# A gated delta rule layer on one core: output with tokens on partitions, both halves of an inverse grown by direct products, paired kk products

## The reference

```python
beta = sigmoid(x @ w_b) * 2.0
g = -exp(A_log) * softplus(x @ w_a + dt_bias)
q, k, v = (conv_silu(x @ w, conv) for w, conv in ...)   # causal, 4 taps
q, k = l2norm(q), l2norm(k)
# per token, per head:
S = S * exp(g_t)
delta = (v_t - k_t @ S) * b_t
S = S + outer(k_t, delta)
o_t = (q_t * 64 ** -0.5) @ S
# then
rms = o * rsqrt(mean(o * o, axis=-1) + EPS)             # over the 128 values of a head
y = (rms * norm_w * silu(x @ w_g)) @ w_out              # w_out sums over all heads
x = x + layernorm(y)
```

## Time and profile before

| | |
|---|---|
| median of 3 runs | 5447.15 us (5446.64 to 5448.37) |
| the profiled execution | 5446.22 us |
| its span, first to last instruction | 5445.0 us |
| busy share PE / DVE / ACT / POOL | 96% / 85% / 55% / 55% |
| delta rule phase, first product to last addition | 144.65 to 4969.3 us |
| before it (norm, gates) | to 128.7 us and the change of phase |
| behind it (experts) | 4970.7 us to the end |

### The profile page before, as it was taken

One profiled execution on the slowest core, in us unless ns is written; L12 is line 12 of the kernel. 1 busy time (PEld: TensorE's weight loads), 2 busy tenths in 40 slices (PEclk: granted clock), 3 DMA queues, 4 the chain that ended last, 5 costly groups with the idle time before them and its releaser, 6 DMA issues. The chain is left out here.

```text
span 5445.0 us, 144552 instructions
## 1 busy us (share of the span) xinstructions
PE 5217.2 (96%) x43532; PEld 3837.1 (70%) x43532; DVE 4620.5 (85%) x10938; ACT 3001.3 (55%) x7772; POOL 2971.6 (55%) x3857
## 2 busy tenths in 40 slices
PE   6899999999999999999999999999999999996998
PEld 6577777777777777777777777777777777774554
DVE  5688888888888888888888888888888888885776
ACT  1456656566566566566566566566665665662221
POOL 3455555555555555565565555555555555553443
PEclk9899999999999999999999999999999999998998
DMA  3111011011011011011110110111110110100110
GB/s 132 40 38 37 27 44 37 27 37 42 29 37 37 27 44 37 28 37 36 36 37 28 40 40 27 37 37 35 37 37 27 42 39 27 37 29 23 39 39 31
DMA packets 114337, 203.67 MB, mean 37 GB/s; under 512 B 12377, under 2 KB 70882, under 8 KB 114274
## 3 DMA queue, kind: packets, MB, share of 16 engines
q1 hardware_dynamic: 114274, 202.90, 11.0%
HBM read 185.56 MB, written 17.30 MB: 37 GB/s over the span
## 5 line engine op out<-in xcount | busy, mean ns | idle before, releaser
L647 DVE SCALAR_TENSOR_TENSOR cv<-ps_a,wqkv,cv 128x511 f32<-128x511 f32 (+2 forms) x1536 | 1115.7, 740 | 21.6 <-ACT cv L640 21.3
L632 PE MATMUL ps_a<-xin,wqkv 128*128 128x512 f32 x2048 | 1011.1, 616 | 48.2 <-issue 28.5
L843 POOL TENSOR_TENSOR bm<-bat,mask 128x256 f16<-128x256 f32 x1536 | 1034.5, 689 | 0.0
L1063 POOL TENSOR_TENSOR rms<-msq,minus_half 128x2 f32<-128x2 f32 x512 | 359.8, 703 | 1065.0 <-DVE msq L1055 1064.9
L904 DVE TENSOR_TENSOR tt<-tt,b 128x256 f16<-128x256 f16 x1536 | 624.5, 414 | 209.5 <-PE b L898 197.1
L914 ACT CAST tt<-b 128x256 f16<-128x256 f32 x1536 | 546.4, 374 | 435.9 <-PE b L909 435.9
L892 ACT ACTIVATE m<-b 128x256 f16<-128x256 f32 x1536 | 549.1, 385 | 308.9 <-PE b L887 308.8
L838 POOL TENSOR_TENSOR tt<-bat,first 128x512 f16<-128x512 f32 x256 | 297.0, 1160 | 757.0 <-DVE tinv L937 756.9
L640 ACT ACTIVATE cv<-ps_a,wqkv 128x512 f32<-128x512 f32 x512 | 351.9, 687 | 546.5 <-PE ps_a L632 546.5
L898 PEld LDWEIGHTS b<-tt,m 128*128 128x128 f16 x6144 | 348.2, 101 | 422.8 <-issue 347.4
L1070 PE MATMUL cz<-wout,yy 128*128 128x256 f32 x2048 | 568.3, 400 | 0.0
(11 more groups left out here) (202 smaller groups left out, 11852.6 us busy)
## 6 DMA issues: line engine op xcount, KB each, us to landing
xin<-xT_scratch SPq DMA_DIRECT2D x128, 512.0 KB, 3.6
grow<-g_scratch SPq DMA_DIRECT2D x128, 512.0 KB, 4.3
gam<-g_scratch SPq DMA_DIRECT2D x256, 96.0 KB, 2.8
n_x<-in_x SPq DMA_DIRECT2D x16, 512.0 KB, 3.3
xT_scratch<-n_xT SPq DMA_DIRECT2D x16, 512.0 KB, 2.6
e_x<-in_x SPq DMA_DIRECT2D x16, 512.0 KB, 4.1
out_y<-e_yo SPq DMA_DIRECT2D x16, 512.0 KB, 2.9
wqkv<-in_w_qkv SPq DMA_DIRECT2D x32, 128.0 KB, 3.4
```

Source lines behind the costliest of these rows:

```text
L632: ins = pe.matmul(ps[:], wqkv[:, k, j * P:(j + 1) * P], xin[p][:, k, :], start=k == 0, stop=k == KT - 1)
L647: s.done(dve.scalar_tensor_tensor(y[:, r:], ps[:, 0:T - r], tap[:, j, TAPS - 1 - r:TAPS - r], y[:, r:], ALU.mult, ALU.add), f"a_tap{j}{r}")
L843: s.done(pool.tensor_tensor(half_of(bm[:, l, units(g), :], l, 1), half_of(bt[:, units(g), :], l, 1), half_of(c["mask"][:, l, :].unsqueeze( ...
```

## The change

- `c_O` swaps its operands, so that its output has tokens on partitions. `c_sq` is then two ACT squares, each of one head, with a running sum along the row into `msq`; the `c_ss` products go. `c_m` and `c_p` are both on POOL. `c_y` multiplies each head with its own `rms` and the gate, `c_yT` transposes both heads on PE (into the second half of bank `co`), `c_yTe` copies on ACT, and `c_out` sums both heads in PSUM, in a bank of `ps_a`. One addition, `c_acc`, is left of two operations.
- The gate is computed with tokens on partitions too: `b_g` has eight matmuls of 256 columns instead of four of 512.
- `norm_w` and its constant go into w_out once, in the gates phase: all of w_out is loaded, scaled on POOL and stored to `wo_scratch`.
- A level of the inverse has the products `b_M`, `b_V` and `b_U`. `b_V` gives the new half of the transpose directly and is added by DVE (`b_Ve`). `b_U` writes a bank of its own, `bu`, shared by both groups; with ones on the diagonal of `m1` it holds the whole new half and is copied by ACT (`b_Ue`). `b_Tp` and `b_Te` go.
- `b_F` also adds the matrix itself by a product with the identity, and `b_T` is a copy on ACT instead of an addition on DVE.
- `b_kk` of a group is one step: for each chunk the products of both row halves follow each other.
- `ck` and `cz` become one bank, `cs`. Bank `co` is now held from `c_O` to `c_yTe`.
- The order of a slot is written anew.

```diff
-    c_y0.3 b_sq1.2 a_proj0.1 a_tap13.1 b_gend.2 b_Me00.2 b_U00.2 c_ss0.3 b_Ue00.2 b_Me51.3 b_n1.2 c_KS1.3 b_U51.3
...
+    b_kT.1 b_V40.2 b_U11.2 a_tap32.1 b_Ve11.2 c_yTe1.3 c_SU2.3 a_tap33.1 b_bm31.2 b_sq0.1 c_O2.3 b_Ve40.2 b_M21.2
+    b_n0.1 b_Ue11.2 b_bm41.2 c_S2.3 a_tanh3.1 b_U40.2 a_silu3.1 b_lo0.2 b_M50.2 b_Me21.2 b_Me50.2 b_Ue40.2 c_sq2.3
+    b_V21.2 c_KS3.3 c_m2.3 b_U21.2 b_ss.1 b_Ve21.2 b_V50.2 c_out1.3 c_R3.3 b_Ue21.2 b_Ve50.2 c_p2.3 b_M31.2 c_Z3.3
+    b_U50.2 c_acc0.3 c_acc1.3 b_rc.1 b_P0.2 c_y2.3 b_kk0.1 b_gam.1 c_u3.3 b_w1.1 b_R0.2 b_kw.1 b_ktok.1 c_yT2.3
+    b_Ue50.2 b_Me31.2 b_ev00.1 b_V31.2 b_Ve31.2 b_ev01.1 b_F0.2 b_bm51.2 c_yTe2.3 b_U31.2 b_Ue31.2 b_root.1 b_qT.1
+    b_eps.2 b_sq1.1 c_O3.3 c_sq3.3 c_out2.3 c_acc2.3 b_diag0.1 c_m3.3 b_t20.1 c_p3.3 b_kk1.1 b_M41.2 b_T0.2 b_n1.1
+    c_Z0.2 b_Me41.2 b_vT0.1 b_bm00.1 c_u0.2 b_ev10.1 b_Tq0.1 b_U41.2 b_hi0.1 b_V41.2 b_Ue41.2 b_vtok0.1 a_proj0
+    c_y3.3 b_Tf0.1 b_Ve41.2 b_M00.1 b_M51.2 c_yT3.3 b_ev11.1 b_vT1.1 b_vtok1.1 b_bm10.1 b_Me00.1 c_SU0.2 b_V00.1
+    b_U00.1 b_Ve00.1 b_Me51.2 c_yTe3.3 b_V51.2 c_out3.3 c_O0.2 b_Ve51.2 c_S0.2 b_Ue00.1 b_M10.1 a_cv0 b_P1.2
+    b_U51.2 c_sq0.2 b_Ue51.2 c_acc3.3 c_KS1.2 a_tap01 b_Me10.1 a_proj1 b_gend.1 b_R1.2 b_F1.2 a_tap02 b_V10.1
+    c_R1.2 b_sel c_m0.2 c_p0.2 b_U10.1 a_tap03 b_E0 b_diag1.1 a_cv1 c_y0.2 a_tanh0 b_g0.1 b_Ue10.1 b_t21.1 c_Z1.2
+    c_yT0.2 b_T1.2 b_bm20.1 b_Ve10.1 a_tap11 a_silu0 a_tap12 b_tg0.1 b_Tq1.1 b_M20.1 b_bm01.1 c_u1.2 b_bm30.1
+    a_tap13 a_proj2 b_Tf1.1 b_Me20.1 b_U20.1 b_kqs.1 b_sg0.1 a_tanh1 a_silu1 c_yTe0.2 b_V20.1 c_SU1.2 a_cv2 b_M01.1
+    b_Ue20.1 b_bm40.1 c_O1.2 b_Ve20.1 a_tap21 a_tap22 b_M30.1 b_Me01.1 c_S1.2 b_E1 b_g1.1 b_bm50.1 b_V01.1 b_Me30.1
+    a_tap23 c_sq1.2 b_Ve01.1 b_U30.1 b_tg1.1 b_V30.1 b_Ve30.1 c_m1.2 a_tanh2 b_bm11.1 a_proj3 b_hi1.1 b_M40.1
+    b_Ue30.1 c_p1.2 c_KS2.2 b_sg1.1 a_silu2 a_cv3 c_y1.2 c_R2.2 b_Me40.1 b_M11.1 b_U01.1 b_Ue01.1 c_out0.2 c_Z2.2
+    c_yT1.2 b_lo1.1 b_Me11.1 b_V11.1 a_tap31 c_u2.2 b_bm21.1
...
+        nc.sync.dma_start(wo[:], w_out.rearrange("n p h d -> p n (h d)")).then_inc(s_wo, 16)
+        nc.sync.dma_start(normw[:], norm_w).then_inc(s_wo, 16)
+        nc.gpsimd.wait_ge(s_wo, 32)
+        nc.gpsimd.tensor_scalar(wo[:], wo[:], normw[:, 0:1], 0.5 * DV ** 0.5, ALU.mult, ALU.mult).then_inc(s_ws, 1)
...
+        nc.sync.wait_ge(s_ws, 1)
+        nc.sync.dma_start(wo_dram.rearrange("n p h d -> p n (h d)"), wo[:]).then_inc(s_out, 16)
+        nc.sync.wait_ge(s_out, 32)
...
+            [(f"b_U{l}{g}", f"b_Ue{l}{g}") for l in range(NLEV) for g in range(2)],
+            [(f"c_KS{m}", f"c_R{m}") for m in range(1, CH)] + [(f"c_Z{m}", f"c_u{m}") for m in range(CH)]
+            + [(f"c_SU{m}", f"c_S{m}") for m in range(CH - 1)],
+            [(f"c_O{m}", f"c_yTe{m}") for m in range(CH)],
...
+                    for m in range(2):
+                        t = slice((2 * n + m) * P, (2 * n + m + 1) * P)
+                        for k in range(KT):
+                            ins = pe.matmul(ps_b[:, m * 2 * DV:(m + 1) * 2 * DV], xin[p][:, k, t], wg[:, k, :],
+                                            start=k == 0, stop=k == KT - 1)
...
+                        for k in range(2):
+                            rows = slice(k * DK, (k + 1) * DK)
+                            ins = pe.matmul(ps_a[k][:, n * 2 * P:(n + 1) * 2 * P], kq[p][rows, 1 - p, t],
+                                            kq[p][rows, :, t], start=True, stop=True)
...
+                    if (yield f"b_V{l}{g}"):
+                        s.need(pe, i, f"b_Me{l}{g}", f"b_Ue{l - 1}{g}" if l else f"b_t2{g}")
+                        for k in range(4):
+                            u = 4 * g + k
+                            ins = pe.matmul(half_bank(bank, l)[:, k], tt[:, 1, u, :], half_of(m1[:, l], l, 0)[:, u],
                                             start=True, stop=True)
...
+                        s.done(dve.tensor_tensor(even, even, half_bank(bank, l), ALU.add), f"b_Ve{l}{g}")
...
+                        pe.matmul(bank[:, k * P:(k + 1) * P], r16[:, u, :], tt[:, 1, u, :], start=True, stop=False)
+                        ins = pe.matmul(bank[:, k * P:(k + 1) * P], tt[:, 0, u, :], c["ident16"][:], start=False,
+                                        stop=True)
...
+                    if (yield f"b_U{l}{g}"):
+                        s.need(pe, i, f"b_Me{l}{g}", f"b_Ue{l - 1}{g}" if l else f"b_t2{g}")
+                        free(pe, i, f"b_U{l}{g}")
...
+                        s.done(act.copy(half_of(tt[:, 1, units(g), :], l, 1), half_bank(bu, l)), f"b_Ue{l}{g}")
...
+                                pe.matmul(co[:, e], kqs[p][:, q_in, m - 1, :], state[:, h, :], start=True, stop=False)
+                            ins = pe.matmul(co[:, e], at[:, 2 * m + h, :], uu[:, h, :], start=m == 0, stop=True)
...
+                    for h in range(2):
+                        ins = act.activation(sqo[:, h, :], out[:, h * DV:(h + 1) * DV], ACT.Square, accum_out=col(msq, h))
...
+                    s.done(pool.tensor_tensor(rms[:, both], msq[:, both], epsq[p][:, both], ALU.add), f"c_m{m}")
...
+                        ins = dve.scalar_tensor_tensor(yy[:, h, :], out[:, e], col(rms, h), sg[p][:, m, e], ALU.mult,
+                                                       ALU.mult)
...
+                        ins = pe.transpose(turned[:, h * P:(h + 1) * P], yy[:, h, :], c["ident"][:])
...
+                        ins = pe.matmul(ps_a[m % 2][:, 0:D], yT[:, h, :], wo[:, h, :], start=h == 0, stop=h == 1)
...
+                    s.done(dve.tensor_tensor(a, a, ps_a[m % 2][:, 0:D], ALU.add), f"c_acc{m}")
...
+        for l in range(NLEV):
+            odd = lambda t: t.rearrange("p u (b k r) -> p u b k r", k=2, r=2 << l)[:, :, :, 1, :]
+            ident = c["ident16"][:].unsqueeze(1)
+            for u in range(NU):
+                ins = pool.tensor_copy(odd(m1[:, l, u:u + 1, :]), odd(ident))
```

More of the change, by code:

```diff
@@ L63 @@
[L63 to L67, removed]
@@ L470, in __init__ @@
                 before = []
+                self.turn.setdefault(first, []).append(before)
                 for d in range(1, 3 * len(users) + 1):
@@ L474, in __init__, with phase_delta @@
                     before.append((LAG[first] - LAG[other[0]] + wraps, other[1]))
-                self.turn[first] = before
     def free(self, eng, i, name):
[L479 to L485, removed]
+        for before in self.turn[name]:
+            for shift, last in before:
+                if not isinstance(i, int) or 0 <= i + shift < NIT:
+                    self.s.need(eng, i + shift, last)
+                    break
+def phase_delta(nc, c, w_qkv, w_gate, wo_dram, xT_dram, g_dram, gate_tok, acc):
     with Phase(nc) as ctx:
@@ L557, in phase_delta @@
         for g in range(2):
[L558 removed]
+            for name in ("b_M", "b_Me", "b_V", "b_Ve", "b_U", "b_Ue", "b_bm"):
                 s.series(f"{name}.{g}", [f"{name}{l}{g}" for l in range(NLEV)])
[L560 to L561 removed]
         for j in range(4):
@@ L567, in phase_delta @@
             s.series(name, [f"{name}{m}" for m in range(CH - 1)])
-        for name in ("c_Z", "c_u", "c_O", "c_sq", "c_y", "c_ss", "c_out", "c_m", "c_p", "c_acch", "c_acc"):
+        for name in ("c_Z", "c_u", "c_O", "c_sq", "c_m", "c_p", "c_y", "c_yT", "c_yTe", "c_out", "c_acc"):
             s.series(name, [f"{name}{m}" for m in range(CH)])
-        sp.dma_start(normw[:], norm_w).then_inc(s.sem("normw_in"), 16)
         def load_x(i, b, par):
@@ L933, in invert @@
                     s.done(ins, f"b_F{g}")
                 if (yield f"b_T{g}"):
-                    s.need(dve, i, f"b_F{g}")
-                    s.need(dve, i - 2, f"c_Z{2 * g + 1}")
-                    s.done(dve.tensor_tensor(tinv[p][:, units(g), :], tt[:, 1, units(g), :], in_units(bank), ALU.add),
-                           f"b_T{g}")
+                    s.need(act, i, f"b_F{g}")
+                    s.need(act, i - 2, f"c_Z{2 * g + 1}")
+                    s.done(act.copy(tinv[p][:, units(g), :], in_units(bank)), f"b_T{g}")
@@ new lines, in emit @@
+                if (yield f"c_m{m}"):
+                    s.need(pool, i, f"c_sq{m}", "b_eps")
+                    s.need(pool, i - 1, f"c_y{m}")
+                    s.done(pool.tensor_tensor(rms[:, both], msq[:, both], epsq[p][:, both], ALU.add), f"c_m{m}")
+                if (yield f"c_p{m}"):
+                    s.need(pool, i, f"c_m{m}")
+                    s.done(pool.tensor_tensor(rms[:, both], rms[:, both], c["minus_half"][:, 0:2], ALU.pow), f"c_p{m}")
+                if (yield f"c_y{m}"):
+                    s.need(dve, i, f"c_p{m}", f"b_sg{m // 2}")
@@ L1042, in emit @@
-                if (yield f"c_ss{m}"):
+                        s.need(dve, i - 1, f"c_yT{CH - 1}")
+                    for h in range(2):
+                        e = slice(h * DV, (h + 1) * DV)
+                        ins = dve.scalar_tensor_tensor(yy[:, h, :], out[:, e], col(rms, h), sg[p][:, m, e], ALU.mult,
```

(8 more changed lines are left out.)

219 lines of the change are left out of this document (89 added, 130 removed).

## The result

The changed kernel takes 5516.7 us (median of 4 runs, 5516.0 to 5521.6) against 5446.9 for the kernel before beside it: a ratio of 1.0131, 95% interval 1.0113 to 1.0148. It is 1.3% slower, with an interval clear of 1, and the forecast of 5278 is missed, outside the range. With 24 waits a trip fewer on ACT, and every operation as in the changed kernel, the same code takes 5267. What the prediction left out is not an operation but the program itself: ACT's part of the loop body came to be fetched from memory again in each trip of the loop (a trip is two iterations, since the code is written out for both parities; there are 61).

The account below looks back on a forecast made before the run. PE's stream was taken to bound the kernel: terms of -1.53 us an iteration, 196 us in 128, and +27 us once give 5446.2 - 196 + 27 = 5277, so 5278 as the runs' median; range 5195 to 5395.

Parts of the forecast that it names:

- the part on the other engines: DVE, ACT and POOL per iteration: 29.4, 26 or so and 22.3 us, all beside PE's stream and priced at nothing.
- PE waits at c_O for the copy yTe: Sign of being wrong: PE waits over 1 us an iteration, above all at c_O for yTe.
- the output chain holding co: Rival: co, held longer, delays the next c_O and all behind it; 5533 us at 2 us late, chance 0.07.
- the four hand-offs: Handing co to the next c_O: 3 us of queueing allowed at the tightest; decisive if together 1.3 us late an iteration.
- The rival of the clock: Rival: added PE transposes lower the clock; 1.2 GHz for a tenth of the loop costs about 450 us, chance under 0.01.
- DVE didn't set the pace: Rival, here denied: DVE and not PE sets the pace, so time follows DVE's 3.6 us to 5012, chance 0.02.
- The rival of the waits: Rival: PE's waits eat most of the gain, leaving 0.1 to 1.0 us an iteration; 5345 to 5440 us, chance 0.17.
- Kk, sums, transposes and identity: Terms on PE's stream per iteration: paired kk -1.15, sums of squares -1.76, transposes of yy +0.88, identity in b_F +0.48 us.
- more than the stream: Rival: PE's old 0.45 us of waits also go, conditions cost nothing, early stages grow by 10 only; 5190 us, chance 0.10.
- the inverse's products: Term on PE's stream: 12 levels keep 12 matmuls of 64 columns for each product, so nothing changes.
- a term of its own: PE's wait at c_O3 for uu goes, -0.39 us an iteration; its counterpart at b_V21 adds +0.39, up to +0.8.
- Once: Stages before the loop: w_out load 8, later store 9, copies into m1 10; together +27 us, from 10 to 45.

Follow-up runs that it names:

- e5: The changed kernel, loop untouched, with 70 long-met waits (35 instructions) on ACT ahead of the first slot: 5268.3 us.
- e2: The changed kernel with the copy b_Ue waiting only for the later of its two products, ACT's body 261 instructions instead of 285: 5267.3 us.
- e7: e2 with the gate rows grow issued ahead of the load of wo in SP's queue: 5238.9 us.
- e4: The kernel before with 96 long-met waits a trip added on ACT, its body 273 instructions instead of 225: 5465.3 us.
- e9: The kernel before with the 96 waits a trip of e4 and 204 more (102 instructions) on ACT ahead of the first slot: 5597.3 us.
- e12: The changed kernel with 20 long-met waits (10 instructions) on ACT ahead of the first slot, where e5 has 70: 5399.5 us.

## Why the prediction was wrong

**The step that failed** is in the part on the other engines: ACT goes from 22.5 us an iteration to 26 or so, lies beside PE's stream, and is priced at nothing. The operations were priced rightly: 315 records of the addition into acc, four an iteration, make 78.8 iterations in the 3000 us, and ACT's 2006.76 us are 25.5 in each. The instructions were not counted, waits and register operations among them, and no step of the working asked whether a loop body is still held when it grows. That step is worth +248 us (e5 against the changed kernel, with the same loop in both), and it turns -180 into +70.

The Trainium skill (Runtime: NRT & Kernel Launch, Instruction fetch mechanics) would have given the warning: it says that a taken branch whose target isn't in the present window of two pages of 16 KiB forces a fetch before the engine can go on. The runs agree on the stall and on its place behind the branch. They differ in grain: here the packets have 8 KB, a body of 285 instructions (18 KB) fell out of what the skill gives as 32 KiB, and one of 312 on DVE did not.

**The signs and the rivals.** "PE waits at c_O for the copy yTe" came as written, with "over 1 us an iteration" (192 us idle in 78.8 iterations are 2.4). The rival that it stood for, the output chain holding co, named the victim and not the culprit; its price of 5533 is near the result for another reason. With the fetches off (e2), no wait of c_O for yTe is left in the view, so the four hand-offs stay within the 3 us that were allowed. The rival of the clock, in with slower at under 0.01, was looked for in the transposes. The clock did fall, behind the standstill of each trip, and took up to 2 of the 4.0 us between 75.2 and 71.2. DVE didn't set the pace either: in e2 it is busy 84% of the time, and the iteration is 35.6 us and not near DVE's 30. The rival of the waits is priced at 5345 to 5440, but its own lower waste of 0.1 us gives 5446 - 13 + 27 = 5460; e2 lies below both.

**The stream.** e2 is the change without the fetches, and its 35.6 us an iteration stand against a forecast of 35.8, its 5267 against 5278. But the terms are off in both directions. The distances from each record's start to the next on PE, summed by line over 80 iterations of the kernel before and 72 of e2 (all of 1000 to 4000 us but the long trips), in us an iteration (a wait counts with the record ahead of it):

```
                          before   e2     by this   forecast
kk                         3.19    2.13    -1.06     -1.15
c_ss                       1.78    -       -1.78     -1.76
yT transposes              -       0.96    +0.96     +0.88
identity in b_F            -       0.45    +0.45     +0.48
M, U and Tp / M, V and U   5.61    4.76    -0.85      0
c_out (wait of kk behind)  3.78    4.69    +0.91      0
b_vT                       1.12    0.87    -0.25      0
all                       37.29   35.60    -1.69     -1.53
```

Kk, sums, transposes and identity are right within 0.1; kk is two blocks of 1.07 us as said (2176.63 to 2177.70), a yT group 0.22 (2166.24 to 2166.46). Two things were not foreseen. The order's new bank sharing lets b_kk1 wait for DVE's c_acc2, 0.83 us an iteration in the waits view and 0.99 by the starts; I had counted waits for b_V and c_O, but not gone through the new list of banks for first users right behind last ones. On the other side, waits of the kernel before went. The first a_proj of a trip came 0.61 us late (the "issue" line of the earlier trace rows), 0.30 an iteration, and a U group behind b_vT 0.21 late; neither does in e2. The working left these to a rival, *more than the stream*.

The line of the inverse's products needs care, for it holds waits of other steps. U took 2.12 us in the kernel before, where 12 groups of 0.12 are 1.44, but 0.39 of the rest is c_O3 waiting for uu behind the last U. The forecast has that as a term of its own, and its counterpart came as written: in e2 b_V21 comes 0.41 us late behind b_M21, forecast 0.39. What else the line lost, beside the wait of a_proj, are steps of about 0.1 us each from an f16 group to an f32 group, fewer now (those into kk the forecast has in its first line). So the inverse's products themselves changed nothing, as forecast; whether its shorter chain bought anything, no run shows. The unforeseen wait and the unforeseen gains nearly cancel, so that 35.8 came out right by some luck.

**DVE and POOL.** DVE is at 30.1 us an iteration (2375.73 in 78.8), foreseen 29.4. Additions into acc take 419 ns, c_y 337 where I had 0.32 us, b_T on ACT 588 instead of 0.62 us:

```profile
L1075 DVE SCALAR_TENSOR_TENSOR yy<-co,rms,sg 128x128 f32<-128x128 f32 x630 | 185.9, 337 | 16.1 <-POOL rms L1066 16.1
...
L1058 ACT ACTIVATION_READ_ACCUMULATOR sqo<-co 128x1 f32 x632 | 133.8, 212 | 0.0
L1100 DVE TENSOR_TENSOR acc<-acc,ps_a 128x256 f32 x315 | 132.1, 419 | 158.0 <-PE ps_a L1095 158.0
...
L948 ACT COPY tinv<-b 128x512 f32<-128x512 f32 x158 | 92.9, 588 | 0.0
```

**Once.** The first w_qkv product comes at 167.56 us, 22.9 later than before, foreseen 27: 8.4 for the later store of g, where I took 8; 5.9 for the store of wo behind it, where I took 9; 8.6 for the copies, where I took 10. What I didn't see is the order in SP's queue: 7 long trips, 28 us (e7). Every queue past which a step is moved has to be checked, and so b_sel's, which the new order runs a slot earlier; I looked at the steps that the diff's functions change and not at those whose lag alone changes.

## What to carry to other kernels

When an edit adds instructions to an engine, count that engine's whole loop body, waits included, and not only its busy time; after the run, look at the instruction queue first: packets in the steady loop were here the sign that a body was fetched again in every trip. The cure can be a handful of waits fewer, or a few instructions ahead of the loop that move the body against its blocks; measure the position too before you call an edit slow. And for every step whose lag changes, go through the queue that feeds it and the bank that it takes over, even where its own code is unchanged.

## What the runs showed of the hardware that was not expected

- A loop of one and the same body costs 248 us more or less by its place in the program: ACT's body of 285 instructions was fetched again (five packets of 8 KB a trip) or not at all, with 35 instructions ahead of it. A body of 273 likewise (e4 and e9, 132 us).
- The engine stands behind its branch for 3.3 us in the changed kernel, 2.4 in e12 and 2.3 in e9 (there 1.1 once more), by where the body lies.
- The wait of PE of some 2.5 us at the head of a trip was followed by 1.2 GHz in all of 40 trips; that of 1.5 us in e12 in 4 of 41.
- A sum taken by ACT with its square is a second operation, 212 ns each, and it adds instructions.
- Met waits are cheap: 48 and 96 a trip in the kernel before cost 11 and 18 us in 61 trips, 3 to 4 ns each; 24 a trip more or less in the changed kernel made no difference (e5 and e2).
